# GATv2 attention layers: rectified chunks joined in pairs on VectorE and GpSimd ahead of the head sums

## What is computed

```python
hs = (x @ Ws + bs).reshape(N, H, HD)
hd = (x @ Wd + bd).reshape(N, H, HD)
e = jax.nn.leaky_relu(hs[src] + hd[dst], SLOPE)      # SLOPE = 0.2
logits = jnp.einsum('ehd,hd->eh', e, attn)
...
alpha = ex / s[dst]                                  # softmax over the edges of a destination
out = jax.ops.segment_sum(alpha[..., None] * hs[src], dst, num_segments=N)
```

## Time and profile before

| what | value |
|---|---|
| median of 3 runs | 2538.82 us (2535.26 to 2540.85) |
| profiled execution, time | 2538.38 us |
| profiled execution, span | 2536.7 us |
| TensorE busy | 2185.9 us, 86% of the span |
| VectorE busy | 1466.3 us, 58% |
| ScalarE busy | 998.3 us, 39% |
| GpSimd busy | 696.3 us, 27% |
| DMA, mean over 16 engines | 160 GB/s over the span; 237 GB/s and a share of 0.79 in the attention stretch 700 to 1050 us |

### The profile page before, as it was taken

One profiled execution on the slowest core, in us unless ns is written; L12 is line 12 of the kernel. 1 busy time (PEld: TensorE's weight loads), 2 busy tenths in 40 slices (PEclk: granted clock), 3 DMA queues, 4 the chain that ended last, 5 costly groups with the idle time before them and its releaser, 6 DMA issues. The chain is left out here.

```text
span 2536.7 us, 95528 instructions
## 1 busy us (share of the span) xinstructions
PE 2185.9 (86%) x33973; PEld 1763.1 (70%) x33974; DVE 1466.3 (58%) x3955; ACT 998.3 (39%) x2619; POOL 696.3 (27%) x749
## 2 busy tenths in 40 slices
PE   6998877996799999999991399599999999998059
PEld 3664444554799999999991155389999999997047
DVE  5225984333566666666667433366666666666882
ACT  2100011221455655655553022156555555564222
POOL 0000001000444454445440000244454445442000
PEclk9999988998899999999996699799999999998579
DMA  5001024211778777777773211477777877874331
GB/s 171 1 1 63 13 82 117 78 60 57 237 238 239 237 238 239 236 239 238 239 211 75 101 55 58 147 211 237 238 237 238 238 237 239 238 235 132 75 112 55
DMA packets 163333, 405.26 MB, mean 160 GB/s; under 512 B 46073, under 2 KB 100636, under 8 KB 162852
## 3 DMA queue, kind: packets, MB, share of 16 engines
q0 software_dynamic: 58432, 298.63, 39.0%
q1 hardware_dynamic: 103069, 101.15, 13.4%
q10 hardware_dynamic: 1764, 4.60, 0.6%
HBM read 368.18 MB, written 16.78 MB: 152 GB/s over the span
## 5 line engine op out<-in xcount | busy, mean ns | idle before, releaser
L614 POOL DMA_INDIRECT at_rows<-table,at_index x728 | 687.5, 944 | 1237.7 <-DVE at_index L810 791.5
L633 ACT ACTIVATE at_relu<-at_turned 128x512 f32<-128x512 f32 x1092 | 635.7, 600 | 613.9 <-PE at_turned L692 588.4
L692 PE MATMUL at_turned<-ident,at_rows 128*128 128x128 f32 x4368 | 822.3, 279 | 0.9 <-issue 0.9
L690 PE MATMUL at_turned<-at_place,dst_rows 96*128 96x128 bf16 x4368 | 791.4, 222 | 6.6 <-DVE at_place L767 6.3
L692 PEld LDWEIGHTS at_turned<-ident,at_rows 128*128 128x128 f32 x4368 | 628.4, 144 | 47.4
L690 PEld LDWEIGHTS at_turned<-at_place,dst_rows 96*128 x4368 | 455.6, 106 | 47.9 <-issue 47.9
L806 DVE SCALAR_TENSOR_TENSOR sums<-sums,at_factor,at_total 128x97 f32 x1456 | 344.9, 310 | 240.8 <-PE at_total L722 240.7
L796 DVE TENSOR_TENSOR at_spread<-at_lined,at_weight 128x1024 f32<-128x1024 f32 x182 | 223.0, 1225 | 234.9 <-ACT at_weight L643 234.9
L722 PE MATMUL at_total<-at_rows,at_spread 128*32 128x100 f32 x11648 | 289.0, 251 | 2.6 <-DVE at_spread L796 2.6
L704 PE MATMUL at_heads<-at_relu,at_attn_mask 128*8 128x128 f32 x8736 | 272.5, 273 | 0.0
L722 PEld LDWEIGHTS at_total<-at_rows,at_spread 128*32 128x32 f32 x11648 | 248.6, 110 | 24.6 <-DVE at_spread L796 2.7
(11 more groups left out here) (282 smaller groups left out, 2191.2 us busy)
## 6 DMA issues: line engine op xcount, KB each, us to landing
at_place<-local_rows SPq DMA_DIRECT2D x182, 96.0 KB
at_rows<-table,at_index POOLq DMA_INDIRECT x728
at_flags<-run_flags SPq DMA_DIRECT2D x182, 64.0 KB
dst_rows<-pr_parts SPq DMA_DIRECT2D x240, 48.0 KB, 1.9
table<-pr_src_row SPq DMA_DIRECT2D x20, 400.0 KB, 2.4
el_moved<-sums SPq DMA_DIRECT2D x64, 120.0 KB, 2.6
mx_w<-in_L_mix_W_qkv SPq DMA_DIRECT2D x2, 2304.0 KB, 19.3
pr_w<-in_L_gnn_Wsrc SPq DMA_DIRECT2D x2, 2304.0 KB, 12.6
```

The lines of the kernel that those rows point to most:

```text
L614: pool.indirect_dma_start(rows[b][:, j, :], None, table, bass.IndirectOffsetOnAxis(index[b][:, j:j + 1], 0)).then_inc(gathered[b], 16)
L633: act.activation(relu[c][:], turned[chunk(b, c)][:], ACT.Relu).then_inc(bent, 1)
L690: pe.matmul(into, dst_rows[:, bass.ds(at[j], 1), c * P:(c + 1) * P].rearrange("p o d -> p (o d)"), place[b][:, j * P:(j + 1) * P], start=T ...
L692: last = pe.matmul(into, rows[b][:, j, c * P:(c + 1) * P], ident[:], is_transpose=True, start=False, stop=True)
```

## The change

ScalarE now rectifies each chunk with a scale for each partition, at_attn_size = |attn|, so relu(|a| v) = |a| relu(v) and only the sign of attn is left. Two chunks of one macro can then be added, once the first is multiplied by the product of both signs (at_pair_sign): chunks 0 and 1, 2 and 3 (`JOINED`) on DVE, one scalar_tensor_tensor for each pair; chunks 4 and 5 (`BESIDE`) in two steps, the multiplication on ScalarE (`sign`, between factors and the bend of chunk 5) and the addition on POOL (`join`, between the gathers j = 2 and j = 3). TensorE multiplies only the three sums, with at_sign_mask (0.8 * sign): 12 products of line 704 in place of 24. On DVE build_place moves from the slot's start to a place ahead of spread_out. New waits: TensorE on `joined` (twice) and `joined_beside`, POOL on `bent` of chunk 5 and on `signed`.

```diff
+JOINED, BESIDE = ((0, 1), (2, 3)), (4, 5)
...
             @block.gpsimd
             def _(pool):
+                def join(m):
+                    from_, c = BESIDE
+                    pool.wait_ge(bent, m * KC + (BANKS + c + 1))
+                    pool.wait_ge(signed, m + 1)
+                    pool.tensor_tensor(relu[c][:], relu[from_][:], relu[c][:], ALU.add).then_inc(joined_beside, 1)
...
+                        if paced and j == 2:
+                            join(m - 2)
...
-                    act.activation(relu[c][:], turned[chunk(b, c)][:], ACT.Relu).then_inc(bent, 1)
+                    act.activation(relu[c][:], turned[chunk(b, c)][:], ACT.Relu, scale=attn_size[:, c:c + 1]).then_inc(bent, 1)
+
+                def sign(m):
+                    from_, c = BESIDE
+                    act.wait_ge(bent, m * KC + (BANKS + from_ + 1))
+                    act.activation(relu[from_][:], relu[from_][:], ACT.Identity, scale=pair_sign[:, c:c + 1]).then_inc(signed, 1)
...
                     if turn:
+                        sign(turn[0])
                         bend(turn[0], turn[1], 5, first)
...
-                    for c in range(KC):
-                        pe.wait_ge(bent, m * KC + (BANKS + c + 1))
+                    for k, (_, c) in enumerate(JOINED):
+                        pe.wait_ge(joined, m * len(JOINED) + (k + 1))
                         for j in range(G):
-                            last = pe.matmul(head_row(j), attn_mask[:, c, :], relu[c][:, j * P:(j + 1) * P], start=False, stop=c == KC - 1)
+                            pe.matmul(head_row(j), sign_mask[:, c, :], relu[c][:, j * P:(j + 1) * P], start=False, stop=False)
+                    pe.wait_ge(joined_beside, m + 1)
+                    for j in range(G):
+                        last = pe.matmul(head_row(j), sign_mask[:, BESIDE[1], :], relu[BESIDE[1]][:, j * P:(j + 1) * P], start=False, stop=True)
                     last.then_inc(heads_done, 1)
...
+                def join(m):
+                    for from_, c in JOINED:
+                        dve.wait_ge(bent, m * KC + (BANKS + c + 1))
+                        dve.scalar_tensor_tensor(relu[c][:], relu[from_][:], pair_sign[:, c:c + 1], relu[c][:], ALU.mult, ALU.add).then_inc(joined, 1)
...
-                    if after:
-                        build_place(*after)
                     if head:
                         line_up(head[0], fresh)
+                        join(head[0])
...
                         first_maximum(head[0])
+                    if after:
+                        build_place(*after)
+                    if head:
                         spread_out(head[0], head[1])
```

More of the change, by code:

```diff
@@ L530, in attend @@
         relu = [sb(f"at_relu{c}", [P, ME]) for c in range(KC)]
-        attn_col, attn_mask, attn_rows = sb("at_attn_col", [P, KC]), sb("at_attn_mask", [P, KC, H]), sb("at_attn_rows", [KC, P])
+        attn_size, attn_sign, attn_rows = sb("at_attn_size", [P, KC]), sb("at_attn_sign", [P, KC]), sb("at_attn_rows", [KC, P])
+        pair_sign, sign_mask = sb("at_pair_sign", [P, KC]), sb("at_sign_mask", [P, KC, H])
         flags = [sb(f"at_flags{b}", [P, 2, P], BF16) for b in range(UNROLL)]
@@ L553, in attend @@
              "firsts", "ends_loaded", "merge_ready", "merged", "merge_seen")]
+        joined, joined_beside, signed = (nc.alloc_semaphore("at_" + s) for s in ("joined", "joined_beside", "signed"))
         gathered = [nc.alloc_semaphore(f"at_gathered{b}") for b in range(UNROLL)]
@@ L556, in attend @@
         flags_loaded = [nc.alloc_semaphore(f"at_flags_loaded{b}") for b in range(UNROLL)]
-        sems += [*names, *local_loaded, *flags_loaded]
+        sems += [*names, joined, joined_beside, signed, *local_loaded, *flags_loaded]
         def chunk(b, c):
@@ L615, in gather @@
                                                 bass.IndirectOffsetOnAxis(index[b][:, j:j + 1], 0)).then_inc(gathered[b], 16)
+                        if paced and j == 2:
+                            join(m - 2)
                 for b in range(UNROLL):
                     gather(b, b, paced=False)
+                for m in range(2):
+                    join(m)
                 with pool.Fori(1, LOOPS) as i:
@@ L623, in _ @@
                     gather(m, m % UNROLL)
+                join(NM - 2)
+                join(NM - 1)
                 for b in range(UNROLL):
@@ L665, in slot @@
                     if turn:
+                        sign(turn[0])
                         bend(turn[0], turn[1], 5, first)
                 act.sem_inc(bent, BANKS)
+                act.wait_ge(attn_ready, 1)
                 slot(macro(0, 0), None, first=True)
@@ L838, in _ @@
                 dve.wait_ge(attn_turned, 1)
-                step(dve.tensor_scalar(attn_col[:], back[:, 0:KC], 1.0 - SLOPE, None, ALU.mult))
+                step(dve.tensor_scalar(attn_size[:], back[:, 0:KC], -1.0, None, ALU.mult))
+                step(dve.tensor_tensor(attn_size[:], back[:, 0:KC], attn_size[:], ALU.max))
+                step(dve.tensor_scalar(attn_sign[:], back[:, 0:KC], 0.0, None, ALU.is_ge))
+                step(dve.tensor_scalar(attn_sign[:], attn_sign[:], 2.0, -1.0, ALU.mult, ALU.add))
+                for from_, c in (*JOINED, BESIDE):
+                    step(dve.tensor_tensor(pair_sign[:, c:c + 1], attn_sign[:, from_:from_ + 1], attn_sign[:, c:c + 1], ALU.mult))
                 for c in range(KC):
-                    step(dve.tensor_scalar(attn_mask[:, c, :], head_mask[:], attn_col[:, c:c + 1], None, ALU.mult))
+                    step(dve.tensor_scalar(sign_mask[:, c, :], head_mask[:], attn_sign[:, c:c + 1], 1.0 - SLOPE, ALU.mult, ALU.mult))
                 dve.sem_inc(scanned, SCANS)
```

## The result

The changed kernel takes 2683.68 us (median of 4 runs, 2682.46 to 2685.96), the kernel before 2537.04 us in the same comparison: a ratio of 1.058, 95% interval 1.0558 to 1.0604. It is 147 us slower. The prediction had 2653 us, 115 us slower, in a range of 2571 to 2750.

The account below looks back on a forecast made before the run. TensorE was taken to bound the kernel at 7.58 us a macro. Bend 5 at T+6.57, release 0.15, addition 1.20, then 0.05 and 0.24 give 8.21 us; 0.63 x 182 = 115 us more makes 2653 us, range 2571 to 2750.

Parts of the forecast that it names:

- Cover: VectorE's two joins, 1.5 us a macro, cost nothing because they fit its waits of 1.29 and 1.33 us.
- The chain: Per macro, bend 5, release, POOL addition and last four products run in sequence; next turning at T+8.21, period 0.63 us longer.
- T: Zero of time in a slot: sum_heads of one macro has been issued and turning of the next begins.
- bend 5: ScalarE's last bend of a macro, chunk 5: ends at T+6.57 in place of T+5.50.
- release: Between the end of bend 5 and the start of POOL's addition: 0.15 us, at most 0.46.
- addition: POOL's sum of chunks 4 and 5: 1.20 us, bounds 0.60 and 1.44.
- from its end to the next T: After POOL's addition: 0.05 us to TensorE and 0.24 us for the last four products.
- L729's wait: TensorE before chunk 5's products stands idle for POOL's addition about 1.35 us in each macro.
- the small steps: Once a layer, beside the loads that the stage starts with: below 3 us in all, left out.
- Rival 4: TensorE's clock falls to half speed because it now idles; the kernel passes 3600 us; 2 in 100.
- Rivals 1 to 3: POOL addition cheap, 2525 us, 5 in 100; ScalarE scale free too, 2430 us, 4; POOL dearer, 2753 us, 16 in 100.

Follow-up runs that it names:

- cover_only: Kernel before, with only a scale by partition (ones) on every ScalarE bend and build_place moved ahead of spread_out: 2541.30 us, ratio 1.0012.
- beside_before: Kernel before, with three spare multiplications of 128x144 a macro on GpSimd that nobody waits for: 2541.06 us, ratio 1.0008.
- two_pairs: Changed kernel without sign and GpSimd addition, chunks 4 and 5 multiplied each by itself: ratio 0.9788 to the kernel before, repeats 0.9750 and 0.9751.
- changed_b: The changed kernel unaltered, repeated on a slower chip: 2981.85 us, ratio 1.0645 to the kernel before.
- no_sign_b: Changed kernel with ScalarE's multiplication of chunk 4 by the pair sign left out, second run: 2884.55 us, ratio 1.0297 to the kernel before.

## Why the prediction was right

**Cover.** TensorE was the bound and all else had slack: shown by cover_only and beside_before, both within 0.3% of the kernel before. The joins on VectorE are free: the wait for messages went from 240.7 to 6.6 us (one of them is in the earlier trace rows), and two_pairs, which keeps them, is faster than the kernel before. 745 ns each against the 750 taken.

**The chain.** Step by step, forecast and measured from T: bend 5 ends 6.57 and 6.43; release 0.15 and 0.07; addition 1.20 and 1.26 (1.27 in the mean); from its end to the next T 0.29 and 0.53 (to the start of the products 0.05 and 0.06, for them 0.24 and 0.47). Sum 8.21 and 8.29. The sum is closer than its terms: two were 0.24 and 0.06 us too low and two 0.14 and 0.08 too high, and that they nearly cancel is luck. So, in part, is the price of the addition, a choice between two bounds for which no run had a number. The bends have 0.69 us, as forecast, and sign 0.76 against 0.72. But the three bends that run back to back push what follows by 0.11 us and not 0.27, so the factors start at T+4.50 in place of T+4.66: that is the earlier bend 5. The Trainium skill, "GPSIMD Engine Reference", section "Elementwise — side-by-side cycle accounting", gives by its figures an estimate of 1.17 us; the trace has 1.27, and 2.09 ns an element where its 2.6 cycles make 2.17. The rate agrees within 4%, and the estimate was 0.1 us low.

The forecast of L729's wait, 1.35 us, was too high. The profile has 1.05 in this slot (194.2 us over 180 waits, 1.08 in the mean). TensorE's earlier work is issued by T+6.63, as forecast (T+6.62), but the last of it is booked as busy for 0.14 us more, and the products start at T+7.82 and not T+7.97.

**Where the missing 32 us are.** Of the 147 us the prediction's sum had 115; the two profiled spans differ by 145. From the starts of spread_out in order of time (180 intervals in the two layers, sum 1367.7 us before and 1500.4 after) the attention slots account for 133 us. Regular slots are 8.28 us on average, against 7.58: 0.70 in place of 0.63, 126 us (the rest are 10 us of long slots after, less 3 us of slow first slots before). The term that was mis-sized most is the end of the chain: four products after a wait take 0.47 us until the next turning, where I took the 0.24 us of four in a running stream. Why they take longer was not tried. It is partly offset by a bend 5 that was earlier than reckoned.

Those 10 us are nine slots of 8.9 to 10.4 us, at six places, about one in 26 slots. GpSimd has a pause there, a gather that starts late:

```profile
864.26 0.95 POOL L623 DMA_INDIRECT at_rows<-table,at_index  x1 [0.30 <-issue]
868.22 1.25 POOL L623 DMA_INDIRECT at_rows<-table,at_index  x1 [3.02 <-DVE at_spread L826]
869.78 0.95 POOL L623 DMA_INDIRECT at_rows<-table,at_index  x1 [0.30 <-issue]
870.75 1.27 POOL L611 TENSOR_TENSOR at_relu<-at_relu 128x512 f32<-128x512 f32 x1
```

3.96 us from one gather to the next, where it is 1.3 elsewhere; the spread that the profile names is not what this gather waits for in the program. In the kernel before it is 3.83 us at 846, 1043 and 1240 us, one in 26 slots too, and no slot is longer for it. With the addition behind gathers in the same queue it now reaches TensorE. That step was missing: I had counted POOL's load over a slot, not its pauses. What makes the pause was not tried.

The last 12 us lie ahead of the first spread of a layer (2.8 us in the first layer; 318.6 against 309.1 us between the last spread of one layer and the first of the next), which I had put below 3 us and left out. In the second layer TensorE waits once 3.42 us for the first join, and the small steps are 1.3 us longer. The last section has what held up that join.

**Rival 4, in miniature.** I gave 2 in 100 to a falling clock. In the profiled run it stays at 1.00 in the stage at large (0.99 in the second layer, from 1900 to 2400 us), but in four of these six places it does fall. One of them (columns of rows 2):

```profile
872.00:874.00 2.00, 1.87 (x24) 0.93 0.71 211
874.00:876.00 2.00, 2.00 (x14) 0.50 0.78 216
876.00:878.00 2.00, 2.00 (x19) 0.71 0.82 259
878.00:880.00 2.00, 2.00 (x72) 1.00 0.57 172
```

It happened after TensorE had stood idle 1.90 us in front of L729 (its usual wait is 1.05), came back by 878, and it is part of the 10 us above. On the slower chips the same fall is common, and costs more (changed_b, above). Rivals 1 to 3 fall: an addition of 1.27 us is neither cheap nor 1.44, the scale is not free (0.69 us a bend against 0.60), and the release is 0.07 us. What stays open is the cause of the pauses on the slower chips, and with it the absolute time of two_pairs on the first. It is the fastest version seen, 2.1 to 2.5% below the kernel before where it ran.

## What to carry to other kernels

Before work is moved off the busiest engine, follow what the remaining part waits for, from its last input to its first use, and compare the sum with the slack in order of time, not with busy shares: here 0.72 us of TensorE's work was exchanged for 2.3 us (0.93 on ScalarE, 1.34 on GpSimd with its release) on a path with 1.1 us to spare (T+5.50 to T+6.62). Two pairs joined where an engine idles anyway gained 2.1 to 2.5%; the third, handed over ScalarE and GpSimd behind the last chunk, lost more than all three saved. Put such a handover on the earliest inputs, or leave the last ones as they are.

## What the runs showed of the hardware

VectorE's int32 copy of the gather indices doesn't finish while GpSimd adds. In a long slot it had 1.01 us instead of 0.17:

```profile
871.04 1.01 DVE L840 COPY at_index<-src_index 128x4 int32 x1
```

GpSimd's addition beside it ended at 872.02. In the whole trace of the changed kernel 173 of these copies overlap an addition, and each ends 0.02 to 0.14 us after the addition does, never before it. The same was seen once with a bf16 comparison: at the start of the second layer at_place took 1.38 us instead of 0.34, and ended 0.15 us after the addition. The first join waits for VectorE behind it, which is a part of the 3.42 us above:

```profile
1719.43 1.26 POOL L611 TENSOR_TENSOR at_relu<-at_relu 128x512 f32<-128x512 f32 x1 [1.25 <-ACT at_relu L648]
...
1719.47 1.38 DVE L792 TENSOR_SCALAR at_place<-at_place,node_of 96x512 bf16<-96x512 bf16 x1 [8.13 <-DMA at_place<-local_rows]
```

The f32 adds to sums beside the same additions kept their 309 ns (310 before). The Trainium skill, "GPSIMD Engine Reference", section "Key points", names contention with VectorE instructions in a 2-port mode or with two SBUF inputs. The first half agrees with these rows if those two operations run in such a mode, which the trace doesn't name. For the second half there is a single case: in no_sign_b the second join of the first macro, with two SBUF inputs, overlapped an addition by 0.36 us. The join kept its time (741 ns, 747 for the others), and the addition took 1.49 us in place of 1.28:

```profile
658.36 1.49 POOL L610 TENSOR_TENSOR at_relu<-at_relu 128x512 f32<-128x512 f32 x1 [6.59 <-ACT at_relu L647]
```
